# Value products of a spectral attention layer: GpSimd takes three of eight head groups in every second part

## The reference, cut to what matters

```python
v = _fno_layer(xn, Vcw, Vsw, H, W)              # 32 heads of one image each, spectral weights
...
p_attn = jax.nn.softmax(scores, axis=-1)        # (batch, head, t, s)
av = jnp.einsum('bnts,bnsk->bntk', p_attn, vf)
av = av.reshape(B, nh, T, H, W).transpose(0, 2, 1, 3, 4).reshape(B * T, nh, H, W)
p = _fno_layer(av, Pcw, Psw, H, W)              # sums over the 32 heads, spectral weights again
```

## Time and profile before

| what | us |
|---|---|
| median of 3 runs | 1945.04 (1941.62 to 1947.04) |
| the profiled execution's own time | 1941.3 |
| its span in the trace | 1939.5 |
| value products in it, first VectorE product to the end of the last | 196.4 to 369.2 |

### The profile page before, as it was taken

One profiled execution on the slowest core, in us unless ns is written; L12 is line 12 of the kernel. 1 busy time (PEld: TensorE's weight loads), 2 busy tenths in 40 slices (PEclk: granted clock), 3 DMA queues, 4 the chain that ended last, 5 costly groups with the idle time before them and its releaser, 6 DMA issues.

```text
span 1939.5 us, 30247 instructions
## 1 busy us (share of the span) xinstructions
PE 1658.2 (85%) x11144; PEld 1022.0 (53%) x11144; DVE 1525.4 (79%) x3025; ACT 1027.1 (53%) x1522; POOL 554.2 (29%) x635
## 2 busy tenths in 40 slices
PE   8774777899699989269899999999899999999684
PEld 8650222499689989234444454444444454444342
DVE  5876999737876769779897998878988788884873
ACT  4388000123446244357777766676666766667620
POOL 1342676300074007313581031001271003000533
PEclk9896999999799999679999999999999999999897
DMA  6560345000000014000020012000131011000892
GB/s 171 227 157 12 90 104 111 2 1 1 1 1 1 1 40 142 3 1 1 1 52 25 1 33 44 12 1 12 22 88 31 25 55 55 12 11 2 287 377 105
DMA packets 131855, 112.42 MB, mean 58 GB/s; under 512 B 40192, under 2 KB 109184, under 8 KB 131168
## 3 DMA queue, kind: packets, MB, share of 16 engines
q1 hardware_dynamic: 130176, 107.41, 19.6%
q0 software_dynamic: 1536, 3.08, 0.5%
HBM read 82.37 MB, written 21.88 MB: 54 GB/s over the span
## 4 chain that ended last, share of the span: by engine, by line
PE 60%; DVE 20%; ACT 9%; issue 7%; POOL 1%; DMA 1%; SPq 1%; POOLq 0%; DVEq 0%; ACTq 0%
PE PS L552 5%; PE PS L554 5%; PE PS L553 5%; PE PS L571 5%; PE PS L572 5%; PE PS L573 5%; DVE U L1209 4%; PE PS L1507 4%; PE PS L1516 4%; PE PS L534 4%; ACT V L1723 4%; PE PS L1434 3%; PE PS L1659 3%; ACT Z L812 2%; DVE MI L978 2%
## 5 line engine op out<-in xcount | busy, mean ns | idle before, releaser
L809 ACT ACTIVATE Z<-PS,MI 128x1024 f32<-128x1024 f32 (+2 forms) x288 | 300.0, 1042 | 257.2 <-PE PS L554 220.6
L998 DVE TENSOR_TENSOR DB<-Z 128x1024 f16<-128x1024 f32 (+2 forms) x288 | 332.6, 1155 | 95.7 <-ACT Z L812 52.8
L978 DVE TENSOR_REDUCE MI<-PS 128x1 f32<-128x512 f32 (+2 forms) x576 | 356.5, 639 | 38.0 <-PE PS L534 21.5
L812 ACT ACTIVATE Z<-PS,MI 128x1024 f16<-128x1024 f32 (+2 forms) x288 | 298.3, 1036 | 0.0
L737 POOL TENSOR_SCALAR Z<-U,Z 128x128 f32<-128x128 f32 x104 | 65.3, 639 | 364.4 <-PE PS L573 243.2
L1209 DVE TENSOR_TENSOR U<-A,PS 128x1408 f32<-128x1408 f32 x108 | 166.2, 1611 | 1.6 <-PE PS L1625 1.6
L720 POOL TENSOR_SCALAR U<-U,Z 128x128 f32<-128x128 f32 x128 | 71.9, 577 | 325.8 <-DVE MI L1030 325.8
L1221 POOL TENSOR_TENSOR U<-A,U 128x1408 f32<-128x1408 f32 x36 | 113.8, 3190 | 88.4 <-DVE MI L1985 33.4
L1631 PE MATMUL PS<-U 128*32 128x352 f32 x1152 | 110.9, 481 | 0.1
L571 PE MATMUL PS<-Z,A 128*128 128x512 f16 (+3 forms) x288 | 104.5, 363 | 5.6 <-ACT CST L820 5.6
L1410 POOL TENSOR_SCALAR U<-U,MI 128x128 f32<-128x128 f32 x128 | 56.1, 452 | 183.2 <-DVE V L2081 183.2
(11 more groups left out here) (445 smaller groups left out, 3664.8 us busy)
## 6 DMA issues: line engine op xcount, KB each, us to landing
V<-in_L_ffn_weight SPq DMA_DIRECT2D x16, 1024.0 KB, 11.3
U<-in_L_ffn_weight SPq DMA_DIRECT2D x14, 1024.0 KB, 15.6
A<-x_planes SPq DMA_DIRECT2D x24, 528.0 KB, 9.6
U<-in_x SPq DMA_DIRECT2D x16, 512.0 KB, 4.3
V<-in_x SPq DMA_DIRECT2D x4, 2048.0 KB, 13.9
Z<-in_x SPq DMA_DIRECT2D x16, 512.0 KB, 4.7
out<-U SPq DMA_DIRECT2D x16, 512.0 KB, 3.5
token_rows<-U SPq DMA_DIRECT2D x16, 512.0 KB, 3.7
```

The costliest lines, as they stand in the source:

```text
L809: act.activation(EX32[u % 2][:, 0:w], s, ACT.Exp, scale=SCALE / (QUP * KUP), bias=pb).then_inc(sem("ex_ev"), 1)
L812: act.activation(EHI[u % 3][:, 0:w], s, ACT.Exp, scale=SCALE / (QUP * KUP), bias=pb).then_inc(sem("hi_ev"), 1)
L978: dve.tensor_reduce(bm[:, g % 2, t, k:k + 1], PS[:, 4 + chunk_no[c] % 2, 0:w], AX.X, ALU.max).then_inc(sem("ch_ev"), 1)
L998: dve.tensor_tensor(ELO[u % 3][:, 0:w], EX32[u % 2][:, 0:w], EHI[u % 3][:, 0:w], ALU.subtract).then_inc(sem("lo_ev"), 1)
```

## The change

`NDV = 6` becomes a table by part, `NDVS = (6, 5, 6, 5, 6, 5)`: VectorE forms six groups in parts 0, 2 and 4 and five in parts 1, 3 and 5, GpSimd two and three. There are 99 products on VectorE and 45 on GpSimd; the pool groups are now numbered 0 to 14. TensorE uses the pool groups behind groups 2 and 4 of a part of six, and behind groups 0, 2 and 4 of a part of five (`POOL_BEHIND`). The mode planes of part r + 1 are issued behind the second plane load of part r, no longer behind the first. The waits count by the new tables. The buffers stay as they were.

```diff
-NDV = 6
+NDVS = (6, 5, 6, 5, 6, 5)
+VALUES_DVE = [(r, g) for r in range(NR) for g in range(NDVS[r])]
+VALUES_POOL = [(r, g) for r in range(NR) for g in range(NDVS[r], NQ)]
+POOL_BEHIND = {6: (2, 4), 5: (0, 2, 4)}
...
         def pool_value_products(pool, p):
-            r = p // 2
+            r, g = VALUES_POOL[p]
             pool.wait_ge(sem(f"e_in{p % 2}"), 64 * (p // 2 + 1))
-            if p % 2 == 0:
+            if g == NDVS[r]:
                 pool.wait_ge(sem(f"xr_modes{r % 2}"), 64 * (r // 2 + 1))
...
             def load_modes(r, n):
                 if r >= 2:
-                    sp.wait_ge(sem("y_dve"), 3 * NDV * (r - 1))
-                    sp.wait_ge(sem("y_pool"), 6 * (r - 1))
+                    sp.wait_ge(sem("y_dve"), 3 * sum(NDVS[:r - 1]))
+                    sp.wait_ge(sem("y_pool"), 3 * sum(NQ - n for n in NDVS[:r - 1]))
...
-            for p in range(2 * NR):
-                r, g = p // 2, NDV + p % 2
+            for p, (r, g) in enumerate(VALUES_POOL):
                 if p == 1:
                     sp.wait_ge(sem("once_dve"), MADE["pbar"])
                 if p >= 2:
...
-                if p % 2 == 0 and 1 <= r < NR - 1:
+                if g == NDVS[r] + 1 and 1 <= r < NR - 1:
                     for n in range(4):
                         load_modes(r + 1, n)
...
-            for d in range(NR * NDV):
-                r, g = divmod(d, NDV)
+            p = -1
+            for d, (r, g) in enumerate(VALUES_DVE):
+                p += g in POOL_BEHIND[NDVS[r]]
...
-                    values(YB[d % 2], r, g, q).then_inc(sem("v_dve"), 1)
-                    if g % 3 == 2:
-                        p = 2 * r + g // 3
+                    values(YB[d % 2], r, g, q, g == NDVS[r] - 1 and g not in POOL_BEHIND[NDVS[r]]).then_inc(sem("v_dve"), 1)
+                    if g in POOL_BEHIND[NDVS[r]]:
                         pe.wait_ge(sem("y_pool"), 3 * p + q + 1)
-                        values(YB[2], r, NDV + g // 3, q).then_inc(sem("v_pool"), 1)
+                        values(YB[2], r, VALUES_POOL[p][1], q, g == NDVS[r] - 1).then_inc(sem("v_pool"), 1)
...
-            for d in range(NR * NDV):
+            for d, (r, g) in enumerate(VALUES_DVE):
                 value_products(dve, d)
-                if d % NDV == 1 and d > NDV:
-                    value_sums(d // NDV - 1)
+                if g == 1 and r:
+                    value_sums(r - 1)
```

More of the change, by code:

```diff
@@ L1199, in value_products @@
         def value_products(dve, d):
-            r, g = divmod(d, NDV)
+            r, g = VALUES_DVE[d]
             if g == 0:
@@ L1404, in _ @@
             pool.wait_ge(sem("once_dve"), MADE["pbar"])
-            for p in range(2 * NR):
+            for p in range(len(VALUES_POOL)):
                 pool_value_products(pool, p)
@@ L1626, in spread, with values @@
                           ).then_inc(sem("e_mm"), 1)
-            def values(y, r, g, q):
+            def values(y, r, g, q, stop):
                 for b in range(B):
                     s = slice(32 * b, 32 * b + 32)
-                    mm = pe.matmul(PS[s, 3 * (r % 2) + q, 0:MR], PT[:, g, s], y[:, b, q, :], start=(g == 0), stop=(g == NQ - 1))
+                    mm = pe.matmul(PS[s, 3 * (r % 2) + q, 0:MR], PT[:, g, s], y[:, b, q, :], start=(g == 0), stop=stop)
                 return mm
@@ L1642, in _ @@
                     pe.wait_ge(sem("y_dve"), i + 1)
-                    if i + 2 < 3 * NR * NDV:
+                    if i + 2 < 3 * len(VALUES_DVE):
                         spread(i + 2)
-                    values(YB[d % 2], r, g, q).then_inc(sem("v_dve"), 1)
-                    if g % 3 == 2:
-                        p = 2 * r + g // 3
+                    values(YB[d % 2], r, g, q, g == NDVS[r] - 1 and g not in POOL_BEHIND[NDVS[r]]).then_inc(sem("v_dve"), 1)
+                    if g in POOL_BEHIND[NDVS[r]]:
                         pe.wait_ge(sem("y_pool"), 3 * p + q + 1)
-                        values(YB[2], r, NDV + g // 3, q).then_inc(sem("v_pool"), 1)
+                        values(YB[2], r, VALUES_POOL[p][1], q, g == NDVS[r] - 1).then_inc(sem("v_pool"), 1)
             pe.wait_ge(sem("once_dve"), MADE["mt"])
@@ L1731, in _ @@
             for r in range(NR):
-                act.wait_ge(sem("v_dve"), 3 * NDV * (r + 1))
-                act.wait_ge(sem("v_pool"), 6 * (r + 1))
+                act.wait_ge(sem("v_dve"), 3 * sum(NDVS[:r + 1]))
+                act.wait_ge(sem("v_pool"), 3 * sum(NQ - n for n in NDVS[:r + 1]))
                 act.activation(Z[:, 2, MR * r:MR * r + MR], PS[:, 3 * (r % 2), 0:MR], ACT.Copy).then_inc(sem("k1_ready"), 1)
```

## The result

The changed kernel took 1933.40 us, the median of 11 runs (1928.66 to 1941.37), against 1945.52 for the kernel before, again of 11 runs (1941.62 to 1951.44). The ratio is 0.9935, interval 0.9923 to 0.9947: 0.65% faster. The forecast was 1933.4, range 1927.3 to 1941.7.

A forecast was written before the change was run, and what follows sets the result against it. VectorE was taken to bound the value-product stage. Nine products less, -13.78 us, plus 2.16 of holds gave -11.6 on the profiled 1941.3, thus 1929.7; 3.7 more for the median gave 1933.4, range 1927.3 to 1941.7.

The forecast's parts named there:

- What bounds the kernel, and 13.78 us for nine products: Value products: VectorE sets the stage's length; nine products moved to GpSimd at 1.531 us each save 13.78 us.
- The follow-through of GpSimd: GpSimd's groups followed to each use by TensorE: groups 1 to 3 run without a pause, from 209.12 to 237.59.
- Group 4's planes: Planes loaded behind the mode planes: group 4 starts at 240.2, ends at 249.7, just before TensorE's use at 249.8.
- The lateness that VectorE would not feel: At group 4's use, VectorE first stalls when TensorE is some 0.9 us late.
- The hold of L1997: At five inner value sums, L1997 waits for GpSimd's running product to end: 3 x 0.34 + 2 x 0.57 = 2.16 us.
- The first phase: Sums of part 0: L1997 due at 234.09, GpSimd's product ends at 234.43, a wait of 0.34 us.
- The clock: TensorE's granted clock behind value-sum pauses: no change counted; bounds -0.9 us (no falls) and +1.3 (a fall at all five).
- The sum: -13.78 + 2.16 = -11.6 us on the profiled 1941.3 gives 1929.7; with 3.7 added, a median of 1933.4.
- No hold: Rival: L1997 at the value sums does not wait for GpSimd, or phases miss; median 1931.2 us; chance 0.15.
- Out of step: Rival: L1997 meets a GpSimd product's start, median 1941.7, or group 4's planes come 2 us later, 1935.6; chance 0.19.
- GpSimd as the bound: Rival: GpSimd sets the pace in all six parts; at 4.0 us per product, median 1952.4 us; chance 0.06.
- the sign: GpSimd's product instruction leaving 3.16 to 3.21 us would show the prediction wrong.

The follow-up runs named there:

- the repeated spread: Changed kernel with the spread just ahead of TensorE's pause for the value sums run five times instead of once: 1932.65 us, ratio 0.9937.
- eighteen groups: Changed kernel with five VectorE groups in all six parts, 90 products on VectorE and 54 on GpSimd: 1956.40 us, ratio 1.0047 to the kernel before.
- The control: Changed kernel with two more TENSOR_TENSORs, one operand in PSUM, in each value sum: 1946.76 us, one run.
- the added SBUF instructions: Changed kernel with two more TENSOR_SCALARs from SBUF to SBUF in each value sum: 1947.33 us, one run.

## Why the prediction was right, and where it was not

- **What bounds the kernel, and 13.78 us for nine products: right.** VectorE's row of 24 products has the spacing (36.84 - 1.61) / 23 = 1.532 us, as before; TensorE waits for GpSimd 0.3 us. Doses of three and nine products gave 4.2 and 12.1 us on the medians, 1.40 and 1.35 us each, where 1.53 less the holds and falls was to be expected.
- **The follow-through of GpSimd: right.** Groups 1 to 3 ran without a pause (210.58, 28.50 us), as worked out.
- **Group 4's planes: about right in time, wrong in what ends last.** I had them at 16.2 us behind the mode planes' issue, which was at 225.50 here, thus 241.7. GpSimd started at 240.86, 15.4 us behind it, and the row names TensorE's use of group 3 as its releaser, so the planes were there by then. Only group 9 waited for planes, until 294.33, 15.0 us behind the issue at 279.32, and that too without TensorE noticing. The step took one of the old distances, 14.9 to 16.4 us, for the landing time. The lateness that VectorE would not feel comes out of the step's own terms as 4.59 - 1.61 - 1.99 = 0.99 us, not 0.9; it was not called on.
- **The hold of L1997: right as a mechanism, too large as a term.** L1997 took 0.49, 0.34, 0.46, 0.34 and 1.25 us at the inner sums, where I had 0.7 and 0.9. The five holds were 0.15, 0, 0.11, 0 and 0.90 us (each duration less 0.344): 1.16 in place of 2.16. The first phase was right, a product ending 0.29 us behind L1997's start where I had 0.34. What failed is what I let it cost: I added the wait for the product's end to the whole instruction, but a held instruction ended only 0.20 to 0.21 us behind GpSimd's product, so a wait of 0.29 cost 0.15; the 0.29 us in the earlier trace rows had already said that less than the whole may follow. At the second and fourth sums GpSimd was already idle: at the second its run ended 0.8 us earlier against the start of the stage than I had it, and L1997 came 0.5 us later, behind the first stall. The fifth hold is large because of the clock: behind the fourth sum the double use that frees GpSimd's buffer was one of the slow ones (2.58 us, from 316.87), so GpSimd began its next run at 319.63, 4.90 us behind the start of VectorE's first product after that sum instead of my 3.57, and L1997 met its product earlier. With the repeated spread there was no fall there, the distance was 3.57 again, and the same instruction took 0.48 at the fifth sum. I had counted holds and clock as terms that do not touch each other.
- **The clock: "no change" was wrong for this trace, within the bound given.** Four stalls of 0.49, 0.57, 0.37 and 0.47 us are 1.90, against 0.88: 1.0 more, where I had bounded it at 1.3.
- **The sum.** -13.78 + 1.16 + 1.02 = -11.6; the trace shows -11.1, and the remaining half microsecond isn't placed: VectorE's products took 1615 ns in the median instead of 1610, but the row of 24 has the old spacing. Two mis-sized terms, 1.0 too much for the holds and 1.0 too little for the clock, have cancelled. Two more did behind them: the profiled execution took 1928.66 us, 1.0 below the 1929.7 that I had for it, though its stage was half a microsecond longer than forecast, and the median lies 4.7 above that execution where I had added 3.7. The exact match of the median is luck in these places; that it fell well inside the range isn't.
- **The rivals.** No hold is out: three sums were held, and the experiments show by what. Out of step did not come here, but it is what happened with eighteen groups (L1997 took 2.80 us at four sums). GpSimd as the bound is not reached at 45 products: they kept a spacing of 3.16 us, although the three behind a held L1997 left the 3.16 to 3.21 us that I had named as the sign. The rival's own sum is off by 0.2: 3 x 15 x 0.16 is 7.2, not 7.4. By what it would need I had said a slower GpSimd; the runs show the other way in, more products. At 48 TensorE begins to wait for it, at 54 it sets the pace.

The Trainium skill, "SBUF — State Buffer", section "Who interferes with whom", has a VectorE instruction in a mode that uses two ports wait for the whole GpSimd instruction that started first, and lets one with at most one SBUF input pass if it is in no such mode; TENSOR_SCALAR is among the operations that it says can enter one. L1997, held although it has a single SBUF input, agrees with that. The control agrees with the second half (520 to 522 ns beside GpSimd), and the added SBUF instructions with the first (up to 3.334 us); the 5.91 us below is more than one GpSimd instruction, and there the measurement goes further than the page.

## What to carry to other kernels

Before work is moved to an idle engine, follow its queue at each use and not in the mean: here the same nine products gained 12 us or lost 6, by where one load stood in SyncE's program, and the load order by itself was worth nothing. A TENSOR_SCALAR from SBUF to SBUF on VectorE took up to 3.33 us beside a GpSimd busy with products of 3.2 us, and once 5.91, instead of 0.34; where GpSimd works without a pause, a form with one operand in PSUM was the cheaper one although it is longer alone (0.52 us): 16.7 us with eighteen groups, nothing that can be told from noise with fifteen. Stop adding work before the second engine has none of its slack left: 45 products gained more than 54, and 48 no more than 45 even with the holds taken away.

## What the runs showed that I had not expected

A held instruction does not always get in at the next end of a GpSimd product. With eighteen groups the first one took 5.91 us, from 237.20 to 243.11. The last two products of GpSimd's run of 15 ended at 239.80 and at 242.90 (its row above, 195.77 + 47.13; the one before, read alone, 236.65 + 3.15): L1997 passed over the first of these and ended 0.21 us behind the second, the last of the run. In the same kernel an L1997 of 2.80 us ended with a product inside a run (273.30, 0.20 us behind 269.95 + 3.15 = 273.10). What decides between the two is not settled.

The other is that holds seem to lock in: once GpSimd waits for TensorE and TensorE, through VectorE, for GpSimd, each part repeats the phase of the one before, and 2.80 us came four times, where by chance some would have fallen near an end. That the four come from one repeated phase is read from one trace.
